# A steady state with a ring of three PSUM banks and GpSimd in VectorE's place, in a fused attention and linear layer

## The chip, the core and the metric

The kernel runs on one core of a Trainium2 chip. The metric is the device time of one execution in microseconds (us), the median of three runs. The engines are TensorE (PE, matrix products from SBUF into PSUM), VectorE (DVE), ScalarE (ACT), GpSimd (POOL) and SyncE (SP, which here issues every DMA). Each engine takes its instructions in the order in which they were written; semaphores tie the engines together. PSUM has eight banks of 128 partitions x 512 f32.

## What is computed

The input is x of shape (8, 1024, 256). It is normalised over the last axis; an attention layer and a quantised linear layer both read the result and are added to x:

```python
xn = _layernorm(x, axis=-1)
x = x + attn(xn, Wq, Wk, Wv, Wo, bo) + ffn(xn, weight_q, weight_scale, bias)

# attn: 16 heads of 16, 8 KV heads, so a group is 2 heads
energy = einsum('nqhd,nkhd->nhqk', q, k) + alibi_bias   # -|i-j| * 2**-(h+1)
p = softmax(energy / sqrt(16)); out = einsum('nhqk,nkhd->nqhd', p, v) @ Wo.T + bo
# ffn: int8 quantisation of xn per token, product with int8 weights, scales, bias
x_scale = max(amax(|x|), 1e-6) / 127; x_q = clip(round(x / x_scale), -128, 127)
out = (x_q @ weight_q.T) * x_scale * weight_scale + bias
```

## The kernel before, in words

The 8192 tokens are 64 tiles of 128 (index t). The attention is 64 units (index u): one batch element and one KV head, so two query heads e = 0, 1 over 1024 x 1024 scores. A unit has 8 key blocks c of 128 keys and, with e, 16 slots s = 2c + e. While unit u runs, one tile is prepared (t = u + PREP_AHEAD, 11 ahead) and one finished (u - OUT_BEHIND, 9 behind), so that the steady state does four things together.

**Column blocks** (`col_block`, L919): scores transposed, 128 keys x 512 queries a half h, a half to one PSUM bank. There are two banks, `ps_col[h]`. q and k are split into bf16 parts, so that one bf16 product of 122 rows gives nearly f32 scores; the bias and minus the row maximum are among these rows. The product is issued in four strips of 32 weights (`in_strips`, L880). ACT takes the exp of each half into `probs` (L797), which frees the bank (`exp_done`). POOL multiplies the block on the diagonal by a factor (`weigh_near`, L516).

**pv blocks** (`pv_block`, L936): four f32 products a block c, with the column of sums included, accumulated into `ps_pv`. After block 7, DVE transposes `ps_pv` in 32 x 32 blocks (`turn_pv`, L655, semaphore `pv_read`), and later divides and transposes again (`norm`, L662, semaphore `att_unit_ready`). The next unit's pv block 0 waits for `pv_read`.

**Row blocks** (`row_block`, L887): the scores of later heads (numbers 2u+3 and 2u+4, 8 blocks each, so 16 per unit) with the queries on partitions, 128 x 1024, into `ps_row[qb % 2]`, only for the row maxima. DVE reduces each (`reduce_block`, L631, L635), and a row block waits until the reduce two blocks before is done (`row_max_found`). `split_max` (L638) writes the negated maxima as two bf16 numbers, PE turns them (`turn_max`, L897), ACT keeps them (`keep_max_t`, L774) and SP writes them into rows of q_col (`place_max`, L336).

**Preparation and finishing**: statistics, `normalise`, `find_scale`, `quantise` (DVE, L546 to L585), products in f32 with all 128 weights for q, k, v (`make_qkv`, L829), bf16 for the linear part (`make_lin`, L847), splitting of q and k into three parts (ACT `keep_qkv`, `find_middle`, DVE `find_rest`, POOL `find_low`), and for the finished tile the projection (`project`, L948) and `finish` (DVE, L683). All of them share one bank, `ps_work`, one after the other.

SP's queue for unit u (L407) is, in this order: the next tile of x, att_t of the tile to be finished, the column set of unit u+1 (10 DMAs; it waits until PE has ended the unit before), `place_max` of head 0, `store_out`, `place_max` of head 1, the row set of unit u+3 (10 DMAs, after the scores that used its buffer), `store_parts`, `store_att(u-1)`. PE's first column block of a unit waits for the column set of 14 DMAs, the four of `place_max` among them (L965).

The order of PE's and DVE's work in a unit is written by slots (L961, L692). PE issues the row blocks in pairs after even slots, pv block c-1 or so in odd ones, the projection at s = 6, turning xn at 8, qkv at 10 between the two row blocks, turning xq at 12, the linear product at 14. DVE does two reduces at each even slot, and turn_pv at s = 1, statistics 5, split_max 6, finish, normalise and find_scale 7, quantise 9, find_rest and norm 11, split_max 14, scale_lin 15.

Of the kernel before, what the change touches and what calls it, by code (L numbers as in the profile page):

```python
# [62 lines left out]
PREP_AHEAD = 11  # L63
OUT_BEHIND = 9
RING = 32
# [4 lines left out]
SLOTS = 2 * BLOCKS  # L70

# [22 lines left out]
def build(nc, x, wqk_t, wv_t, wo_t, w8_t, w_scale, bias_attn, bias_lin, q_alibi, k_alibi, diag,  # L94
          eye, parts_dram, att_dram, out):
    ctx = ExitStack()
    with ctx:
# [33 lines left out]
        parts = sb("parts", [P, 2, PARTS, QK_CHUNKS * P], BF16)  # L131
        lin = sb("lin", [P, 2, EMBED])
        v_all = sb("v_all", [P, RING, P])

# [21 lines left out]
        ps_col = [ctx.enter_context(nc.psum_tensor(f"ps_col{i}", [P, HALF], F32)) for i in range(2)]  # L156
        ps_pv = ctx.enter_context(nc.psum_tensor("ps_pv", [P, HALF], F32))
        ps_work = ctx.enter_context(nc.psum_tensor("ps_work", [P, HALF], F32))

        early = [(ps_row[i][:, 0:HALF], ps_row[i][:, HALF:SEQ]) for i in range(2)]  # L160
        work = (ps_work[:, :], ps_work[:, :])

        def last_bank(t):


            banks = [ps_row[i][:, h * HALF:(h + 1) * HALF] for i in range(2) for h in range(2)]
            banks += [ps_col[0], ps_col[1], ps_pv, ps_work]
            return banks[t % BLOCKS][:, 0:EMBED]
# [38 lines left out]
        col_scores = sem("col_scores")  # L207
        exp_done = sem("exp_done")
# [10 lines left out]
        att_last_loaded = [sem(f"att_last_loaded{i}") for i in range(EC)]  # L219
        projected = sem("projected")  # L220
        out_ready = sem("out_ready")
        out_stored = [sem(f"out_stored{i}") for i in range(2)]
# [10 lines left out]
        def wait_apart(eng, s, value):  # L233
# [9 lines left out]
        SEGMENTS = [  # L243
            (0, 1, True, False, False, 2, True),
            (1, OUT_BEHIND, True, True, False, 2, True),
            (OUT_BEHIND, UNITS - PREP_AHEAD, True, True, True, 2, True),
            (UNITS - PREP_AHEAD, UNITS - 3, False, True, True, 2, True),
            (UNITS - 3, UNITS - 2, False, True, True, 2, False),
            (UNITS - 2, UNITS - 1, False, True, True, 1, False),
            (UNITS - 1, UNITS, False, True, True, 0, False),  # L250
        ]
        def run_units(eng, unit):


            for first, end, prep, prev, proj, row_heads, row_set in SEGMENTS:
                flags = dict(prep=prep, prev=prev, proj=proj, row_heads=row_heads, row_set=row_set)
# [18 lines left out]

        def row_banks_spare(f, s):

            return f["row_heads"] == 0 or (f["row_heads"] == 1 and s >= BLOCKS)

        def col_bank(f, s, h):  # L280

            if row_banks_spare(f, s) and s % 2:
                return ps_row[0][:, h * HALF:(h + 1) * HALF]
            return ps_col[h][:, :]
# [5 lines left out]
        def _(sp):  # L290
# [45 lines left out]
            def place_max(u, par, e):  # L336

                wait_apart(sp, max_t_ready, GROUP * u + e + 1)
# [16 lines left out]
            def load_att_t(t, par):  # L355

                wait_apart(sp, att_stored, 16 * GROUP * (t + BLOCKS))
                wait_apart(sp, projected, t)
                sp.dma_start(att_t[:, par, :, :], att_dram[:, bass.ds(t * P, P)].rearrange(
                    "(c p) n -> p c n", p=P)).then_inc(att_t_loaded, 16)  # L360
# [7 lines left out]
            sp.dma_start(base[:, 1:PREP_AHEAD, :],  # L368
                         x[P:PREP_AHEAD * P, :].rearrange("(t p) d -> p t d", p=P)).then_inc(
# [14 lines left out]
            def next_x(t):  # L384

                wait_apart(sp, x_loaded, 16 * (t - PREP_AHEAD))
# [20 lines left out]
            def unit(u, par, f):  # L407
                if f["prep"]:
                    if f["proj"]:

                        wait_apart(sp, out_ready, u - OUT_BEHIND)
                    next_x(u + PREP_AHEAD)
                if f["proj"]:
                    load_att_t(u - OUT_BEHIND, (par + OUT_BEHIND) % 2)
                not_last = not (isinstance(u, int) and u == UNITS - 1)
                if not_last:

                    wait_apart(sp, col_scores, 2 * SLOTS * u)
                    load_col_set(u + 1, 1 - par)
                    place_max(u + 1, 1 - par, 0)  # L420
                if f["proj"]:
                    store_out(u - OUT_BEHIND, (par + OUT_BEHIND) % 2)
                if not_last:
                    place_max(u + 1, 1 - par, 1)
                if f["row_set"]:

                    wait_apart(sp, row_scores, BLOCKS * GROUP * (u + 2))
                    if f["prep"]:
                        wait_parts(u + PREP_AHEAD, (par + PREP_AHEAD) % 2)
                    else:  # L430
                        wait_parts(TILES, 0)
                    load_row_set(u + 3, 1 - par)
                if f["prep"]:
# [10 lines left out]
            load_att_t(TILES - OUT_BEHIND, (TILES - OUT_BEHIND) % 2)  # L444

# [7 lines left out]
            for t in range(TILES - OUT_BEHIND, TILES):  # L453
                sp.wait_ge(out_ready, t + 1)
# [7 lines left out]
        def _(pool):  # L462
# [53 lines left out]
            def weigh_near(u, c):  # L516

                wait_apart(pool, exp_done, 2 * SLOTS * u + 2 * GROUP * (c + 1))
# [3 lines left out]

            def unit(u, par, f):
                t, tpar = u + PREP_AHEAD, (par + PREP_AHEAD) % 2
                for c in range(BLOCKS):
                    weigh_near(u, c)
                    if c == 1 and not (isinstance(u, int) and u == UNITS - 1):
# [3 lines left out]
                    if c == 2 and f["prep"]:  # L531
                        find_rstd(t, tpar)
                    if c == 6 and f["prep"]:
                        find_low(t, tpar)
                if f["prep"]:
                    add_linear(t, tpar)

            run_units(pool, unit)


# [520 lines left out]
```

## Time and profile before

| | |
|---|---|
| median of 3 runs | 1769.76 us (1768.62 to 1770.13) |
| profiled execution | 1769.02 us |
| its span in the trace | 1767.2 us |
| instructions | 68604 |
| mean granted TensorE clock | 0.988 |
| HBM read, written | 101.06 MB, 35.65 MB |

The span is what the trace covers; the profiled execution is 1.8 us longer. A page of the profile gives the busy time of each engine; the chain of waits follows back from the last instruction to what released it; the timeline lists instructions in order of time, merged where they follow each other ("x8" is eight instructions, the second column their common duration). Starts are us from the span's start. Matmul durations include the drain of the array and overlap, so the cost of a matmul on PE is read from the distance of starts or from the chain, not from its duration.

### The profile page before, as it was taken

To read this page: it belongs to the slowest core of one execution; us is meant where nothing else is said; L and a number is where in the kernel's file an instruction comes from. 1 tells how busy PE (TensorE), PEld (TensorE's weight loads), DVE (VectorE), ACT (ScalarE), POOL (GpSimd) and SP (SyncE) were. 2 spreads that over 40 slices of the span, in tenths; PEclk is the share of its full clock that TensorE was granted. 3 is DMA by queue.
4 is the path that set the end of the run, shared out by engine and by line. 5 is a ranking of instruction groups with operands and counts; after the bars stand their busy time and mean duration, and the time that the engine had idled before them with its cause. 6 is when DMAs were issued, how large, how long until landed. Compare 5 with 4: busy or idle time off the path is not lost.

```text
span 1767.2 us, 68604 instructions
## 1 busy us (share of the span) xinstructions
PE 1707.5 (97%) x22272; PEld 719.4 (41%) x22272; DVE 1594.3 (90%) x2306; ACT 1243.0 (70%) x2498; POOL 591.9 (33%) x904
## 2 busy tenths in 40 slices
PE   6799999999999999999999999999999999999997
PEld 4234443443443443443443443443444444333333
DVE  6899999999999999999999999999999999999991
ACT  3267777777777777777777777777777777777775
POOL 4323333333333333333333333333333333222221
PEclk9799999999999999999999999999999999999999
DMA  4322223223223223223223223223233222222222
GB/s 117 86 71 76 65 70 80 71 79 86 75 78 85 76 78 85 75 79 85 75 79 84 74 81 84 74 81 83 75 81 84 74 81 80 71 72 68 72 63 70
DMA packets 184331, 137.99 MB, mean 78 GB/s; under 512 B 102649, under 2 KB 143865, under 8 KB 184281
## 3 DMA queue, kind: packets, MB, share of 16 engines
q1 hardware_dynamic: 184280, 137.34, 28.8%
q8 instruction: 29, 0.48, 0.1%
q14 instruction: 22, 0.17, 0.0%
HBM read 101.06 MB, written 35.65 MB: 77 GB/s over the span
## 4 chain that ended last, share of the span: by engine, by line
PE 69%; DVE 19%; issue 7%; DMA 1%; DVEq 1%; ACT 1%; SPq 1%; POOL 0%; POOLq 0%; ACTq 0%
PE ps_row L884 20%; PE ps_col L884 19%; PE ps_pv L943 18%; DVE row_max L635 13%; PE ps_work L833 5%; PE ps_work L950 3%; DVE att_normed L674 2%; DVE rest L591 2%; PE ps_work L836 1%; PE ps_work L825 1%; PE ps_work L850 1%; ACT probs L797 1%; DVE rsum L667 1%; DMA bias<-bias_lin 0%; DVEq L231 0%
## 5 line engine op out<-in xcount | busy, mean ns | idle before, releaser
L797 ACT ACTIVATE probs<-ps_col 128x512 f32<-128x512 f32 x2024 | 1098.4, 595 | 293.4 <-PE ps_col L884 293.0
L635 DVE TENSOR_REDUCE row_max<-ps_row 128x1 f32<-128x1024 f32 x1024 | 1201.2, 1213 | 64.4 <-PE ps_row L884 62.8
L520 POOL TENSOR_TENSOR probs<-probs,near 128x256 f32<-128x256 f32 x512 | 376.8, 736 | 1074.0 <-ACT probs L797 1074.0
L884 PE MATMUL ps_col<-q_col,k_col 122*32 122x512 bf16 x8096 | 657.0, 383 | 0.5 <-ACT probs L797 0.4
L884 PE MATMUL ps_row<-k_row,q_row 120*32 120x512 bf16 x8192 | 579.0, 386 | 23.2 <-DVE row_max L635 18.2
L943 PE MATMUL ps_pv<-probs,v_unit 128*32 128x512 f32 x4096 | 530.9, 594 | 3.1 <-POOL probs L520 2.9
L884 PEld LDWEIGHTS ps_col<-q_col,k_col 122*32 122x32 bf16 x8096 | 202.7, 94 | 548.3 <-ACT probs L797 428.6
L884 PEld LDWEIGHTS ps_row<-k_row,q_row 120*32 120x32 bf16 x8192 | 193.5, 95 | 212.7 <-DVE row_max L635 139.6
L943 PEld LDWEIGHTS ps_pv<-probs,v_unit 128*32 128x32 f32 x4096 | 119.6, 110 | 82.4 <-issue 11.9
L833 PE MATMUL ps_work<-xn_t,wqk 128*128 128x128 f32 x636 | 85.1, 284 | 0.0
L833 PEld LDWEIGHTS ps_work<-xn_t,wqk 128*128 128x128 f32 x636 | 75.0, 191 | 22.5 <-issue 22.5
L744 ACT ACTIVATE v_all<-ps_work 128x128 f32 (+1 forms) x53 | 14.7, 277 | 89.8 <-PE ps_work L836 89.8
L660 DVE STREAM_TRANSPOSE pv_turned<-ps_pv 128x512 f32<-128x512 f32 x64 | 45.2, 706 | 20.4 <-PE ps_pv L943 20.4
L950 PE MATMUL ps_work<-wo,att_t 128*128 128x256 f32 x224 | 63.3, 405 | 0.0
L781 ACT ACTIVATE neg_max_t<-ps_work 16x128 bf16<-16x128 bf16 x128 | 34.0, 266 | 37.4 <-PE ps_work L899 34.3
L481 POOL TENSOR_TENSOR parts<-rest,parts 128x384 bf16<-128x384 f32 x64 | 59.1, 923 | 0.9 <-ACT parts L753 0.7
L490 POOL TENSOR_TENSOR base<-base,lin 128x256 f32 (+1 forms) x64 | 46.8, 731 | 11.6 <-POOL base L488 11.2
L488 POOL TENSOR_TENSOR base<-base,bias 128x256 f32 (+1 forms) x64 | 47.1, 736 | 9.7 <-DVE lin L598 8.0
L950 PEld LDWEIGHTS ps_work<-wo,att_t 128*128 128x128 f32 x224 | 37.9, 189 | 27.1 <-issue 24.2
L689 DVE TENSOR_TENSOR out_tile<-ps_work,base 128x256 f32<-128x256 f32 x55 | 23.4, 425 | 20.9 <-issue 15.9
L739 ACT ACTIVATE xn_t<-ps_work 128x256 f32<-128x256 f32 x53 | 20.3, 383 | 29.8 <-PE ps_work L825 29.8
L475 POOL TENSOR_TENSOR rstd<-rstd,half_pow 128x1 f32<-128x1 f32 x64 | 35.8, 559 | 11.9 <-POOL rstd L472 11.0
(74 smaller groups left out, 807.4 us busy)
## 6 DMA issues: line engine op xcount, KB each, us to landing
parts_dram<-parts SPq DMA_DIRECT2D x64, 288.0 KB, 3.2
q_row<-parts_dram SPq DMA_DIRECT2D x128, 96.0 KB
q_col<-parts_dram SPq DMA_DIRECT2D x128, 96.0 KB
q_row<-parts_dram SPq DMA_DIRECT2D x128, 64.0 KB
q_col<-parts_dram SPq DMA_DIRECT2D x128, 64.0 KB
att_dram<-att_unit SPq DMA_DIRECT2D x128, 64.0 KB
att_t<-att_dram SPq DMA_DIRECT2D x56, 128.0 KB, 2.2
out<-out_tile SPq DMA_DIRECT2D x55, 128.0 KB, 1.8
```

The costliest lines, as they stand in the source:

```text
L475: pool.tensor_tensor(rstd[:, par, 1:2], rstd[:, par, 0:1], half_pow[:, :], ALU.pow).then_inc(rstd_ready, 1)
L481: pool.tensor_tensor(parts[:, par, 2, :], rest[:, par, :], parts[:, par, 1, :], ALU.subtract).then_inc(low_ready, 1)
L488: pool.tensor_tensor(here, here, bias[:, :], ALU.add).then_inc(base_ready, 1)
L490: pool.tensor_tensor(here, here, lin[:, par, :], ALU.add).then_inc(base_ready, 1)
L520: pool.tensor_tensor(here, here, near[:, bass.ds(u % KV_HEADS, 1), :].rearrange("p a (e n) -> p (a e) n", e=GROUP), ALU.mult).then_inc(wei ...
L635: dve.tensor_reduce(row_max[:, e, qb:qb + 1], ps_row[qb % 2][:, :], AX_X, ALU.max).then_inc(row_max_found, 1)
L660: dve.transpose(pv_turned[:, :], ps_pv[:, :]).then_inc(pv_read, 1)
L797: act.activation(probs[:, c % PBUFS, e, h * HALF:(h + 1) * HALF], col_bank(f, s, h), ACT.Exp, scale=SCALE).then_inc(exp_done, 1)
L833: pe.matmul(bank[:, m * P:(m + 1) * P], wqk[:, c, m * P:(m + 1) * P], xn_t[:, c, :], start=(c == 0), stop=(c == EC - 1))
L884: mm = pe.matmul(to[at, :], weights[:, at], moving, start=start, stop=stop)
L943: mm = pe.matmul(ps_pv[32 * j:32 * j + 32, :], v_unit[:, par, c, :], probs[:, c % PBUFS, j // 2, (j % 2) * HALF:(j % 2 + 1) * HALF], start ...
L950: mm = pe.matmul(bank, att_of_tile[:, c, :], wo[:, c, :], start=(c == 0), stop=(c == EC - 1))
```

## The change

**Ring.** The three banks of ps_col and ps_work become three of one kind, `ps_ring`, and every product of the steady state that isn't a row block or a pv block takes the next of them in a fixed order: 32 column halves and four further items, "early_max" after c = 2, "turns" after 5, "qkv" after 6, "outputs" after 7. An item waits until the item three before it is freed by ACT (`ring_freed`). Turns holds xn, xq and the maxima of head 1; outputs holds the linear product and the projection. ACT copies what it holds to SBUF (`keep_turns`, `keep_qkv_whole`, `keep_outputs`; three, two and two copies) in the order of the ring. Items that have nothing to do in the first or last units are filled and freed by small instructions. The products of the preparation keep their 128 weights; they aren't cut into strips.

**PE's order** in block c: half (e 0, h 0), half (0, 1), row block 2c, half (1, 0), pv block c-2 (for c = 0, 1 blocks 6, 7 of the unit before), half (1, 1), row block 2c+1, and then the further item.

**DVE** keeps two reduces per c (now negated by the reduce itself), and behind them: statistics at c = 0, turn_pv at c = 1, normalise and find_scale at c = 2, norm at c = 3. **POOL** gets split_max, quantise, the split of q and k (`split_qk`, one unit later than before), the weighting of the linear product, and finish. ACT scales the linear product by the token's scale.

**SP's order**: next x (one tile further ahead), att_t, column set, store_parts of the tile before, place_max of head 0, store_att(u-1), row set, store_out of the tile before, place_max of head 1.

```diff
+    others = {2: "early_max", 5: "turns", 6: "qkv", 7: "outputs"}
+    for c in range(BLOCKS):
+        items += [(c, e, h) for e in range(GROUP) for h in range(2)]
+        if c in others:
+            items.append(others[c])
```

In SP's `unit(u, par, f)`:

```diff
+                if not f["last"]:
+
+                    wait_apart(sp, ring_filled, ITEMS * u)
                     load_col_set(u + 1, 1 - par)
+                if f["lag"]:
+                    store_parts(u + PREP_AHEAD - 1, (par + PREP_AHEAD - 1) % 2)
+                if not f["last"]:
                     place_max(u + 1, 1 - par, 0)
-                if f["proj"]:
-                    store_out(u - OUT_BEHIND, (par + OUT_BEHIND) % 2)
-                if not_last:
-                    place_max(u + 1, 1 - par, 1)
+                if f["prev"]:
+                    store_att(u - 1)
                 if f["row_set"]:
                     wait_apart(sp, row_scores, BLOCKS * GROUP * (u + 2))
...
                     load_row_set(u + 3, 1 - par)
-                if f["prep"]:
-                    store_parts(u + PREP_AHEAD, (par + PREP_AHEAD) % 2)
-                if f["prev"]:
-                    store_att(u - 1)
+                if f["out"]:
+                    store_out(u - OUT_BEHIND - 1, (par + OUT_BEHIND + 1) % 2)
+                if not f["last"]:
+                    place_max(u + 1, 1 - par, 1)
```

In POOL's:

```diff
+                if f["prev"] and not f["last"]:
+                    split_max(GROUP * u + 2, 0)
+                if f["lag"]:
+                    split_qk(t - 1, 1 - tpar)
                 for c in range(BLOCKS):
                     weigh_near(u, c)
+                    if c == 0 and f["prep"]:
+                        find_rstd(t, tpar)
+                    if c == 1 and f["lag"]:
+                        weigh_linear(t - 1, 1 - tpar)
+                        add_linear(t - 1, 1 - tpar)
...
                     if c == 2 and f["prep"]:
+                        quantise(t, tpar)
+                    if c == 3 and f["row_heads"] >= 1:
+                        split_max(GROUP * u + 3, 1)
+                    if c == 3 and f["out"]:
+                        finish(u - OUT_BEHIND - 1, (par + OUT_BEHIND + 1) % 2)
```

In DVE's:

```diff
+                for c in range(BLOCKS):
+                    for i in (2 * c, 2 * c + 1):
+                        if i < BLOCKS and f["row_heads"] >= 1:
+                            reduce_block(GROUP * u + 3, 1, i)
+                        if i >= BLOCKS and f["row_heads"] >= 2:
+                            reduce_block(GROUP * u + 4, 0, i - BLOCKS)
+                    if c == 0 and f["prep"]:
+                        wait(dve, x_loaded, 16 * (t - X_AHEAD + 1))
+                        find_stats(t, tpar)
+                    if c == 1 and f["prev"]:
                         turn_pv(u - 1)
+                    if c == 2 and f["prep"]:
                         normalise(t, tpar)
                         find_scale(t, tpar)
+                    if c == 3 and f["prev"]:
                         norm(u - 1)
```

In PE's program:

```diff
+            def take_bank(u, item):
+                if not (isinstance(u, int) and ITEMS * u + PLACE[item] < BANKS):
+                    pe.wait_ge(ring_freed, ITEMS * u + PLACE[item] - BANKS + 1)
+                return ring_bank(item)
+            def unit(u, par, f):
+                for c in range(BLOCKS):
+                    if c == 0:
+                        pe.wait_ge(col_set_loaded[par], 16 * COL_SET * ((u - par) // 2 + 1))
+                    col_half(u, par, c, 0, 0)
+                    col_half(u, par, c, 0, 1)
+                    ahead_row_block(u, par, f, 2 * c)
+                    col_half(u, par, c, 1, 0)
+                    if c >= 2:
+                        pv_block(u, par, c - 2)
+                    elif f["prev"]:
+                        pv_block(u - 1, 1 - par, BLOCKS - 2 + c)
+                    col_half(u, par, c, 1, 1)
+                    ahead_row_block(u, par, f, 2 * c + 1)
```

## Rows read from the trace of the kernel before

**Rows 1.** The page: busy us (share of the span) x instructions, by engine.
```profile
PE 1707.5 (97%) x22272; PEld 719.4 (41%) x22272; DVE 1594.3 (90%) x2306; ACT 1243.0 (70%) x2498; POOL 591.9 (33%) x904
```

**Rows 2.** Chain of waits, 903 to 930 us: start, length, what.
```profile
905.05 2.33 DVE row_max L635 x2
...
907.42 0.61 PE ps_row L884 x8
908.04 0.33 PE ps_work L850 x2
...
908.91 0.86 PE ps_pv L943 x8
...
910.28 0.86 PE ps_row L884 x16
...
919.43 1.06 PE ps_work L950 x4
...
923.28 0.37 PE ps_work L825 x2
```

**Rows 3.** Timeline of DVE in the same unit: start, length, line, operation.
```profile
903.66 0.24 DVE L667 RECIPROCAL rsum<-pv_turned 128x16 f32<-128x16 f32 x1
...
913.14 0.70 DVE L660 STREAM_TRANSPOSE pv_turned<-ps_pv 128x512 f32<-128x512 f32 x1
913.77 2.31 DVE L635 TENSOR_REDUCE row_max<-ps_row 128x1 f32<-128x1024 f32 x2
...
918.55 0.42 DVE L548 BATCH_NORM_STATS2 stats<-base 128x6 f32 x1
...
919.23 2.35 DVE L635 TENSOR_REDUCE row_max<-ps_row 128x1 f32<-128x1024 f32 x2
...
922.72 0.41 DVE L558 TENSOR_SCALAR xn<-base,mean_var,rstd 128x256 f32 x1
...
923.97 2.36 DVE L635 TENSOR_REDUCE row_max<-ps_row 128x1 f32<-128x1024 f32 x2
926.25 0.34 DVE L577 TENSOR_SCALAR xclip<-xn,xinv 128x256 f32<-128x256 f32 x1
...
928.59 1.22 DVE L635 TENSOR_REDUCE row_max<-ps_row 128x1 f32<-128x1024 f32 x1 [0.21 <-PE ps_row L884]
```

**Rows 4.** Timeline of PE, the row blocks on both sides of qkv.
```profile
925.41 0.61 PE L884 MATMUL ps_row<-k_row,q_row 120*32 120x512 bf16 x8
...
927.92 0.62 PE L884 MATMUL ps_row<-k_row,q_row 120*32 120x512 bf16 x8
```

**Rows 5.** DVE's transposes of ps_pv: all, and two of the drain.
```profile
L660 DVE STREAM_TRANSPOSE pv_turned<-ps_pv x64: 703/706/717, 122.0 to 1749.4; 128x512 f32<-128x512 f32 x64
...
1496.87 0.71 DVE L660 STREAM_TRANSPOSE pv_turned<-ps_pv 128x512 f32<-128x512 f32 x1
...
1520.62 0.71 DVE L660 STREAM_TRANSPOSE pv_turned<-ps_pv 128x512 f32<-128x512 f32 x1
```

**Rows 6.** Groups by line: two-input operations of POOL, busy us, mean ns.
```profile
L481 POOL TENSOR_TENSOR parts<-rest,parts 128x384 bf16<-128x384 f32 x64 | 59.1, 923 | 0.9 <-ACT parts L753 0.7
...
L488 POOL TENSOR_TENSOR base<-base,bias 128x256 f32 x60 | 44.1, 735 | 6.8 <-DVE lin L598 5.1
```

**Rows 7.** Timeline of SP's queue, 923 to 938 us.
```profile
923.93 0.40 SPq L440 DMA_DIRECT2D out<-out_tile  x1
925.53 1.35 SPq L340 DMA_DIRECT2D q_col<-neg_max_t  x2
927.77 1.74 SPq L319 DMA_DIRECT2D k_row<-parts_dram  x3
...
934.33 0.31 SPq L326 DMA_DIRECT2D k_row<-k_alibi  x1
...
936.13 1.58 SPq L351 DMA_DIRECT2D att_dram<-att_unit  x2
```

**Rows 8.** The page's DMA issues: KB each, us from issue to landing.
```profile
out<-out_tile SPq DMA_DIRECT2D x55, 128.0 KB, 1.8
```

More of the change, by code:

```diff
@@ L239, in wait_apart, with flags_of @@
                 eng.sem_inc(waited, 1)
[L243 to L251, printed above, removed]
+        SEGMENTS = [(0, 1), (1, OUT_BEHIND), (OUT_BEHIND, OUT_BEHIND + 1), (OUT_BEHIND + 1, 52),
+                    (52, 53), (53, 54), (54, 60), (60, 61), (61, 62), (62, 63), (63, 64)]
+        def flags_of(u):
+            return dict(
+                prep=u + PREP_AHEAD < TILES,
+                lag=0 < u and u - 1 + PREP_AHEAD < TILES,
+                prev=u > 0,
+                proj=u >= OUT_BEHIND,
+                out=u > OUT_BEHIND,
+                next_x=u + X_AHEAD < TILES,
+                row_heads=max(0, min(GROUP, UNITS - 1 - u)),
+                row_set=u + 3 < UNITS,
+                last=u == UNITS - 1,
+            )
         def run_units(eng, unit):
-            for first, end, prep, prev, proj, row_heads, row_set in SEGMENTS:
-                flags = dict(prep=prep, prev=prev, proj=proj, row_heads=row_heads, row_set=row_set)
+            for first, end in SEGMENTS:
+                flags = flags_of(first)
+                assert all(flags_of(u) == flags for u in range(first, end))
                 if end - first == 1:
@@ L800, in unit @@
[L800 to L815 removed]
+                keep_first_max(e)
@@ new lines, in qkv_whole @@
+            def qkv_whole(u, par):
+                t, bank = u + PREP_AHEAD, take_bank(u, "qkv")
+                pe.wait_ge(xn_t_ready, t + 1)
+                for m in range(QK_CHUNKS):
+                    for c in range(EC):
+                        pe.matmul(bank[:, m * P:(m + 1) * P], wqk[:, c, m * P:(m + 1) * P],
+                                  xn_t[:, c, :], start=(c == 0), stop=(c == EC - 1))
+                for c in range(EC):
+                    mm = pe.matmul(bank[:, QK_CHUNKS * P:], xn_t[:, c, :], wv[:, c, :],
+                                   start=(c == 0), stop=(c == EC - 1))
+                mm.then_inc(ring_filled, 1)
@@ new lines, in outputs @@
+            def outputs(u, par, f):
+                t, bank = u + PREP_AHEAD, take_bank(u, "outputs")
+                if f["prep"]:
+                    pe.wait_ge(xq_t_ready, t + 1)
+                    for c in range(EC):
+                        mm = pe.matmul(bank[:, 0:EMBED], xq_t[:, c, :], w8[:, c, :],
+                                       start=(c == 0), stop=(c == EC - 1))
+                if f["proj"]:
+                    pe.wait_ge(att_t_loaded, 16 * (u - OUT_BEHIND + 1))
+                    opar = (par + OUT_BEHIND) % 2
+                    for c in range(EC):
+                        mm = pe.matmul(bank[:, EMBED:2 * EMBED], att_t[:, opar, c, :], wo[:, c, :],
+                                       start=(c == 0), stop=(c == EC - 1))
+                else:
+                    mm = pe.transpose(max_turn(bank), eye_b[:, 0:MAX_ROWS * BLOCKS], eye_b[:, :])
+                mm.then_inc(ring_filled, 1)
@@ L948, in project @@
+            run_units(pe, unit)
+            for c in (BLOCKS - 2, BLOCKS - 1):
+                pv_block(UNITS - 1, (UNITS - 1) % 2, c)
             def project(att_of_tile, bank):
```

401 lines of the change are left out of this document (222 added, 179 removed).

## Prediction

> **What bounds the kernel now.** I read the page's busy line first [rows 1]. TensorE (PE) is busy 97% of the span, VectorE (DVE) 90%, ScalarE (ACT) 70%, GpSimd (POOL) 33%. That says PE and DVE are both near the limit, but not which wait matters, so next I read the chain of waits over one unit of the steady state [rows 2] and DVE's timeline of the same unit [rows 3]. The reader is to see a loop through two engines. A row block (two 512-wide score products in four strips, 0.86/2 = 0.43 us) fills one of two ps_row banks, DVE reduces it, and only then may PE fill that bank again. Three constants of this loop follow. From PE's start of a row block to DVE's start on it: 928.59 - 927.92 = 0.67 us [rows 3, 4]. From one reduce to the next: (926.25 - 923.97)/2 = 1.14 us [rows 3]. From the start of a reduce to the next use of its bank: two reduces started at 905.05, the second ended 2.33 later and PE went on at 907.42, so 2.37 - 1.14 = 1.23, and with the 0.03 that waits add elsewhere I use 1.26 us [rows 2].
>
> The unit's length comes from DVE's transposes of ps_pv, one per unit [rows 3, 5], the first at 122.0: 1496.87 - 913.14 = 583.7 us for 22 units, 26.53 us each. The first 30 take 791.1 us; with 22 of 26.53 the 8 units without projection take 25.9 each. Without preparation a unit takes 1520.62 - 1496.87 = 23.75 us.
>
> PE's own work in a full unit: eight column blocks c, each of four column halves (0.85), two row blocks (0.86) and one pv block (0.86): 2.56 us, so 20.5. Beside them projection 1.06, the linear product 0.33, turning xn 0.37 [rows 2], qkv 927.92 - 925.41 - 0.43 = 2.08 [rows 4], small turns 0.2. Sum 24.5 us; 2 us of the 26.53 are waits.
>
> **The change, DVE and PE.** DVE loses quantise, the splits of the maxima, rest, the scaling of the linear product and finish. What it keeps beside 16 reduces (18.2 us) has four terms [rows 3]: statistics 919.23 - 918.55 = 0.68; the transpose of ps_pv 913.77 - 913.14 = 0.63; normalise and scale 923.97 - 922.72 = 1.25; norm 905.05 - 903.66 = 1.39 [rows 2, 3]. Sum 22.2 us, below PE's 24.5. On the sum alone both engines have room. But the change also moves the terms: all four now stand behind the reduces of c = 0, 1, 2 and 3, while all of PE's extras stand at the ends of c = 5 (turns), 6 (qkv) and 7 (outputs). In c = 0 to 3 DVE has 8 x 1.14 + 3.95 = 13.1 us of work against PE's 10.3, and two banks let DVE lag by one block only. In c = 5 to 7 DVE starves. So I worked the loop through. R is PE's start of a row block, D the start of its reduce, us from the unit's first matmul. Between R of an even and of the next odd block PE does 1.71 us, between odd and even 0.85.
>
> R0 0.43, D0 1.10. R1 2.14, D1 2.81. Statistics push D2 to 4.63; D3 5.77. The transpose runs 6.91 to 7.61. Here a new wait bites: pv block 0 now stands in c = 2 and needs that transpose (pv_read). PE comes to it at 6.53 and is held to 7.66, with row block 5 queued behind it. R5 8.73, D4 7.54, D5 9.40. Normalise and scale to 11.79, D6 11.79, D7 12.93. R8 is wanted at 12.19 and must wait for D6 + 1.26 = 13.05. Norm runs 14.07 to 15.5. D8 15.46, so R10, wanted at 15.61, waits until 16.72. From there PE works alone: R11 18.43, turns 0.52, R12 19.80, R13 21.9, qkv, R14 24.7, R15 26.5, outputs to 28.25. In this stretch 0.5 us is the ring: turns, qkv and outputs occupy ring banks for three, two and two ACT copies at some 0.50 each (1243.0 us over 2498 instructions, [rows 1]), and the third column half behind them needs the bank. So 28.25 us by PE and DVE, where it was 26.53.
>
> What the ring gives: a part of the 2 us of waits is column halves that wait for the exp of their bank; with three banks a half needs the exp of three items back, which at 0.50 each is done. In c = 0 to 3 that gain lies under DVE's loop and vanishes there.
>
> **The change, GpSimd.** POOL takes over quantise (3 operations), the splits (4 short), high, rest and middle of qk (3 of 384 columns), the weighting of the linear product and finish. No row shows one-input operations of these sizes on POOL; from above they are bounded by its two-input ones, 0.73 for 256 columns and 0.92 for 384 [rows 6], from below by half that. With 8 weighings of 0.73, low, add_linear and the rest POOL has between 14 and 20 us per unit; I take 17.5. It fits into 28. What is queued: split_max and split_qk stand in front of weigh_near of c = 0, about 5 us from the unit's start, with weigh_near done near 5.8. Its product pv 0 is due at 6.5 and held to 7.66 anyway. Covered, by 1.9 us. The rows show POOL at 0.73 us for 256 columns of two inputs [rows 6] and DVE at 0.34 for the clip of as many with one, at 926.25 [rows 3]. The Trainium skill, GPSIMD Engine Reference (its introduction and "Elementwise — side-by-side cycle accounting"), calls GpSimd the wrong choice for ordinary elementwise arithmetic, about two times slower than VectorE. DVE gives up about 2.7 us a unit (1594.3/64 = 24.9 [rows 1], less the 22.2 it keeps). By that rule they become an estimated 5.4 on POOL, inside the 14 to 20 that the rows give; the sum is the same by both unless POOL comes late, which is a part of rival B.
>
> ACT loses middle (0.5) and gains two copies of 256 columns (0.8): no bound.
>
> **The change, SP's queue.** This is the step on which the size depends. The first product of a unit waits for its whole column set, of which the last transfers are the maxima of head 1 (place_max(u+1, 1)). Before, these were issued ahead of the row set. Now SP goes: column set, store_parts, place_max 0, store_att(u-1), row set, store_out, place_max 1. store_att waits for norm, and norm stands in c = 3, ready at 15.5 plus 0.1 for waking PE from a DMA: 15.6. Everything queued behind it waits too. Prices [rows 7]: store_att 1.58; the gap of waits in front of the row set 927.77 - (925.53 + 1.35) = 0.89; row set (934.33 + 0.31) - 927.77 = 6.87; store_out 0.40; the first of the two place_max transfers 1.35/2 = 0.67; the second lands about 1.9 after its issue (a transfer to the output 1.8 [rows 8]; none of 2 KB has a row, bounds 1.0 and 3.0); three short gaps of 0.4 (estimate, bounds 0.1 and the 0.89 just named). Sum 13.5 us. Unit: 15.6 + 13.5 = 29.1 us. That is later than PE's own 28.25, so this chain sets the end and PE idles 0.8 us at the head of a unit. The gap fits the other moves: store_parts comes one unit later, and the wait for stored parts ends before 15.6.
>
> **Sum**, against the profiled execution's 1769.0 us (span 1767.2 and 1.8 around it; the median of the runs is 1769.8). Units 9 to 52: 44 x (29.1 - 26.53) = +113. Units 1 to 8, no store_out in the chain: 28.3 against 25.9, 8 x 2.4 = +19. Units 53 to 60, no statistics and no normalise, so norm ends at 14.2, but the row set is still issued: 27.7 against 23.75, 8 x 3.95 = +32. Unit 0 has neither transpose nor norm, -2.5. The last three have no row set, -1. Together +160: 1930 us.
>
> **Rivals.**
> (A) SP's chain is shorter than I price it (landing at 1.0, gaps at 0.1) and PE with DVE sets the unit: 28.25 for units 9 to 52 (+76), 27.2 for 1 to 8 (+10), 23.6 in the drain (-1), -3.5 at the ends. 1851 us. For it: 0.8 us of difference hangs on one landing I can't see. Against: each listed transfer has a measured price.
> (B) A landing of 3 us behind the row set's packets, or POOL late, delaying weigh_near and pv in c = 0 to 3: another 1.0 us for 60 units, 1990 us.
> (C) The other side, faster. Mechanism: DVE's lag is absorbed and PE's work decides, at 24.5 us. It decides only if DVE's c = 0 to 3 fitted beside PE's, and the shortest loop I can write says no: D0 to D8 13.1, to the reuse of the bank 1.26, PE from R10 to the next R0 11.4, and 0.67: 26.4 us, even with no pv_read wait, no idle of DVE between D0 and D1 and no ring wait. So faster asks that a constant of mine is over by 10%. If it did decide: 1769 - 2.0 x 60 = 1650 us.
> (D) The loop at its floor, 26.4, SP hidden: 1765 us, no change.
>
> **How the numbers follow.** Forecast (SP chain) 0.50; A 0.25; B 0.15; C 0.05; D 0.05. The forecast's own range is 1890 to 1965 (landing and gaps at their ends, 0.7 us for 60 units). To leave out 2 in 10 the range goes from 1845, just under A, to 1990, at B. A measurement of this kernel can tell about 0.2% (3.5 us) from no change. Faster: C and a part of D, 0.06. Same 0.03. Slower 0.91.
>
> **What would show it.** In the profile after: PE at the first column half of a unit idle about 1 us, released by the q_col<-neg_max_t transfer; SP waiting about 4 us ahead of store_att in each unit; PE's pv at c = 2 held by pv_turned for about 1 us; row blocks 8 and 10 waiting about 1 us for row_max, none waiting in c = 5 to 7; DVE's busy share near 77%, PE's 84%. If DVE's idle is spread evenly over the unit, or the units without preparation stay at 23.7 us, the argument on SP is wrong. If a full unit is under 26.4 us, the loop is wrong.

## The result

| | before | after |
|---|---|---|
| median | 1769.76 us | 1920.53 us (1918.37 to 1927.12, 4 runs) |
| ratio | | 1.086, 95% interval 1.083 to 1.089 |
| span of the profiled execution | 1767.2 us | 1916.2 us (execution 1918.37) |

The change makes the kernel 8.6% slower. The page after answers to [rows 1]: busy us, share and instructions by engine, and the shares of the chain that ended last.

```profile
PE 1699.2 (89%) x22294; PEld 782.0 (41%) x22294; DVE 1444.1 (75%) x1736; ACT 1273.7 (66%) x2575; POOL 973.6 (51%) x1580
...
PE 27%; SPq 26%; issue 20%; DVE 18%; DMA 6%; DVEq 1%; ACT 1%; POOL 0%; POOLq 0%; ACTq 0%
```

VectorE is relieved as meant, by 150 us of busy time, and yet no engine is busier than PE at 89%. SP's queue, which only issues DMAs, has 26% of the chain. The transposes of ps_pv give the length of the units, as [rows 5] did. Timeline of DVE: units 1, 9, 53 and 61.

```profile
125.57 0.71 DVE L753 STREAM_TRANSPOSE pv_turned<-ps_pv 128x512 f32<-128x512 f32 x1
...
349.94 0.71 DVE L753 STREAM_TRANSPOSE pv_turned<-ps_pv 128x512 f32<-128x512 f32 x1
...
1618.98 0.70 DVE L753 STREAM_TRANSPOSE pv_turned<-ps_pv 128x512 f32<-128x512 f32 x1
...
1839.63 0.71 DVE L753 STREAM_TRANSPOSE pv_turned<-ps_pv 128x512 f32<-128x512 f32 x1
```

Units 1 to 8 take 28.05 us on average (25.9 before), units 9 to 52 28.84 (26.53), units 53 to 60 27.58 (23.88). That is 17 + 102 + 30 = 149 us, as much as the difference of the spans; what comes before the first transpose (3.6 us more) and behind the last (less) nearly cancels.

Timeline of SP in one unit, to be laid beside [rows 7]:

```profile
1015.75 0.32 SPq L358 DMA_DIRECT2D k_col<-k_alibi  x1
1016.43 0.66 SPq L329 DMA_DIRECT2D parts_dram<-parts  x1
1017.73 1.47 SPq L376 DMA_DIRECT2D q_col<-neg_max_t  x2
1023.52 1.55 SPq L387 DMA_DIRECT2D att_dram<-att_unit  x2
1026.05 1.75 SPq L351 DMA_DIRECT2D k_row<-parts_dram  x3
1028.19 4.25 SPq L351 DMA_DIRECT2D q_row<-parts_dram  x6
1032.61 0.31 SPq L358 DMA_DIRECT2D k_row<-k_alibi  x1
1033.22 0.40 SPq L474 DMA_DIRECT2D out<-out_tile  x1
1033.81 1.52 SPq L376 DMA_DIRECT2D q_col<-neg_max_t  x2
```

SP stands idle from 1019.2 to 1023.5 and then issues to 1035.3, with one gap of 1.0 us, in front of the row set, and shorter ones. Timelines of DVE and PE around it, with the idle time in brackets:

```profile
1022.62 0.45 DVE L774 STREAM_TRANSPOSE att_unit<-att_normed 128x256 f32<-128x256 f32 x1
```

```profile
1007.47 0.72 PE L1003 MATMUL ps_ring<-q_col,k_col 122*32 122x512 bf16 x8 [0.32 <-DMA q_col<-neg_max_t]
...
1010.52 0.70 PE L1003 MATMUL ps_row<-k_row,q_row 120*32 120x512 bf16 x8
...
1015.44 1.06 PE L1056 MATMUL ps_pv<-probs,v_unit 128*32 128x512 f32 x8 [1.10 <-DVE pv_turned L753]
...
1020.80 0.61 PE L1003 MATMUL ps_row<-k_row,q_row 120*32 120x512 bf16 x8 [0.39 <-DVE row_max L730]
...
1024.23 0.62 PE L1003 MATMUL ps_row<-k_row,q_row 120*32 120x512 bf16 x8 [0.66 <-DVE row_max L730]
...
1036.50 0.62 PE L1003 MATMUL ps_ring<-q_col,k_col 122*32 122x512 bf16 x8 [0.52 <-DMA q_col<-neg_max_t]
```

The unit starts at 1007.47; norm ends at 1023.07, 15.60 us later; SP's chain ends with PE's start at 1036.50, 13.43 us after that. Inside, PE waits for the transpose at pv block 0 and for reduces at row blocks 8 and 10, as the hand schedule has it.

### The profile page after: what moved, and what is told of

Read it like the earlier page. It is cut to its first block, busy times and chain, and to the rows that moved or that the text cites. A ratio compares the mean times of both kernels' runs of the same rounds, so it can differ in the third digit from the quotient of the medians.

```text
span 1916.2 us, 68781 instructions
## 1 busy us (share of the span) xinstructions
PE 1699.2 (89%) x22294; PEld 782.0 (41%) x22294; DVE 1444.1 (75%) x1736; ACT 1273.7 (66%) x2575; POOL 973.6 (51%) x1580
## 4 chain that ended last, share of the span: by engine, by line
PE 27%; SPq 26%; issue 20%; DVE 18%; DMA 6%; DVEq 1%; ACT 1%; POOL 0%; POOLq 0%; ACTq 0%
SPq L351 16%; PE ps_pv L1056 9%; DVE row_max L730 9%; PE ps_row L1003 8%; PE ps_ring L1003 8%; DMA q_col<-neg_max_t 5%; SPq L387 4%; SPq L376 2%; DVE att_normed L767 1%; DVE amax L660 1%; DVE xn L653 1%; DVE att_unit L774 1%; DVE stats L643 1%; SPq L474 1%; DVE pv_turned L753 1%
## 5 line engine op out<-in xcount | busy, mean ns | idle before, releaser
L865 ACT ACTIVATE probs<-ps_ring 128x512 f32<-128x512 f32 x2048 | 1130.3, 596 | 375.7 <-PE ps_ring L1003 345.2
L1003 PE MATMUL ps_ring<-q_col,k_col 122*32 122x512 bf16 x8192 | 749.2, 382 | 47.6 <-DMA q_col<-neg_max_t 42.1
L1003 PE MATMUL ps_row<-k_row,q_row 120*32 120x512 bf16 x8192 | 645.6, 386 | 73.5 <-DVE row_max L730 63.3
L1056 PE MATMUL ps_pv<-probs,v_unit 128*32 128x512 f32 x4096 | 535.8, 594 | 64.0 <-DVE pv_turned L753 34.2
L1003 PEld LDWEIGHTS ps_ring<-q_col,k_col 122*32 122x32 bf16 x8192 | 234.1, 95 | 413.4 <-ACT probs L865 126.8
L570 POOL TENSOR_SCALAR xclip<-xn,xinv 128x256 f32<-128x256 f32 x53 | 60.9, 1149 | 74.0 <-DVE xinv L666 74.0
L1096 PE MATMUL ps_ring<-xn_t,wqk 128*128 128x128 f32 x636 | 85.1, 284 | 0.0
L1096 PEld LDWEIGHTS ps_ring<-xn_t,wqk 128*128 128x128 f32 x636 | 75.0, 191 | 22.5 <-ACT probs L865 22.5
L753 DVE STREAM_TRANSPOSE pv_turned<-ps_pv 128x512 f32<-128x512 f32 x64 | 45.2, 706 | 25.9 <-PE ps_pv L1056 25.9
L573 POOL TENSOR_SCALAR xround<-xclip 128x256 f32<-128x256 f32 x53 | 57.2, 1079 | 9.8 <-POOL xclip L570 9.5
L1114 PE MATMUL ps_ring<-wo,att_t 128*128 128x256 f32 x220 | 57.7, 385 | 0.0
L586 POOL TENSOR_TENSOR rest<-qk,parts 128x384 f32<-128x384 f32 x53 | 48.8, 921 | 9.5 <-POOL parts L584 9.3
L577 POOL TENSOR_SCALAR xq<-xround 128x256 bf16<-128x256 f32 x53 | 46.1, 870 | 14.5 <-POOL xround L573 14.3
L525 POOL TENSOR_TENSOR base<-base,lin 128x256 f32 (+1 forms) x64 | 46.7, 729 | 13.4 <-POOL base L523 12.9
```

The costliest lines, as they stand in the source:

```text
L570: pool.tensor_scalar(xclip[:, :], xn[:, par, :], xinv[:, par, :], Q_MAX, ALU.mult, ALU.min).then_inc(xq_ready, 1)
L753: dve.transpose(pv_turned[:, :], ps_pv[:, :]).then_inc(pv_read, 1)
L865: act.activation(probs[:, c % PBUFS, e, h * HALF:(h + 1) * HALF], ring_bank((c, e, h)), ACT.Exp, scale=SCALE).then_inc(ring_freed, 1)
L1003: mm = pe.matmul(to[at, :], weights[:, at], moving, start=start, stop=stop)
L1056: mm = pe.matmul(ps_pv[32 * j:32 * j + 32, :], v_unit[:, par, c, :], probs[:, c % PBUFS, j // 2, (j % 2) * HALF:(j % 2 + 1) * HALF], start ...
L1096: pe.matmul(bank[:, m * P:(m + 1) * P], wqk[:, c, m * P:(m + 1) * P], xn_t[:, c, :], start=(c == 0), stop=(c == EC - 1))
```

## Experiments

Theory S says that SP's chain from norm to place_max sets the unit; theory D says that the bunching of DVE's work against PE's extras does. The first three runs bear on the two, one edit each; the fourth prices the third bank.

**e1: store_att behind place_max.**

```diff
-                if f["prev"]:
-                    store_att(u - 1)
                 if f["row_set"]:
...
                     place_max(u + 1, 1 - par, 1)
+                if f["prev"]:
+                    store_att(u - 1)
```

> The changed kernel with one edit: in SP's queue store_att(u-1) moves from ahead of the row set to behind place_max of head 1, so nothing of the next unit's column set waits for norm. Theory S (SP's chain norm, store_att, row set, store_out, place_max sets the unit at 28.84 us, PE and DVE follow at about 28.4): PE no longer waits for q_col<-neg_max_t; full units go to about 28.4, units without projection to 27.3, drain units from 27.6 to about 23.7; total 1863 us. Theory D (the bunched DVE work alone sets the unit, SP's wait is a by-product): full units unchanged at 28.8, total above 1900.

Measured 1869.6 us, 1.056 (1.054 to 1.058) of before. So 51 of the 151 us go when SP no longer waits for norm ahead of the next unit's set. The row for PE's wait on q_col<-neg_max_t, 42.1 us over 57 times after, is gone from the list of waits. Units 9 to 52 take 28.38 us on average (28.34 from the transpose at 1027.60 to the one at 1055.94). So S sets the end, and D stands 0.5 us behind it, which is why the unit gained only so little and the drain, where D gives 24.6 us, gained most: 24 us over 8 units, against 20 over the 44 full ones.

**e2: norm one block later, SP's queue as changed.**

```diff
-                    if c == 3 and f["prev"]:
+                    if c == 4 and f["prev"]:
                         norm(u - 1)
```

> The changed kernel with one edit: DVE's norm(u-1) moves from behind the reduces of c = 3 to behind those of c = 4; SP's queue stays. Theory S: norm ends 2.4 us later, and everything behind store_att with it: about 31.2 us a unit, total near 2065. Theory D: DVE's work of c = 0 to 3 shrinks by 1.39 us, so row block 10 waits no longer and the unit falls to about 27.6, total near 1860. The two have opposite signs against 1920.

Measured 2184.2 us, 1.235 (1.232 to 1.237). The sign is S's and the size nearly twice the forecast, 264 us instead of 145. Timeline of PE, two starts of a unit, then the stretches around the second: us, busy of PE, PEld, DVE, ACT, POOL, granted clock, DMA share, GB/s.

```profile
1004.43 1.15 PE L1003 MATMUL ps_ring<-q_col,k_col 122*32 122x512 bf16 x8 [3.51 <-DMA q_col<-neg_max_t]
...
1010.04 0.66 PE L1003 MATMUL ps_row<-k_row,q_row 120*32 120x512 bf16 x8
...
1038.54 1.04 PE L1003 MATMUL ps_ring<-q_col,k_col 122*32 122x512 bf16 x8 [3.66 <-DMA q_col<-neg_max_t]
```

```profile
1005.00:1010.00 5.00, 5.00 (x48) 2.73 (x42) 1.35 (x2) 2.28 (x4) 0.38 (x2) 0.53 0.36 105
1010.00:1015.00 5.00, 3.78 (x62) 1.79 (x56) 4.84 (x7) 3.85 (x7) 3.02 (x6) 1.00 0.32 89
1015.00:1020.00 5.00, 4.88 (x69) 1.84 (x69) 4.01 (x7) 3.22 (x7) 2.81 (x5) 1.00 0.21 47
...
1035.00:1040.00 5.00, 1.46 (x16) 0.72 (x20) 0.00 (x0) 1.54 (x4) 3.22 (x6) 0.70 0.24 75
1040.00:1045.00 5.00, 5.00 (x54) 1.75 (x48) 2.33 (x2) 2.31 (x5) 0.74 (x1) 0.62 0.38 101
```

The end of norm in between, from DVE's timeline:

```profile
1024.64 0.45 DVE L774 STREAM_TRANSPOSE att_unit<-att_normed 128x256 f32<-128x256 f32 x1
```

This unit is 34.1 us; units 9 to 52 average 33.3. Norm ends at 1025.09, 20.66 after the start instead of the 18.0 expected, and 13.45 later PE starts: SP's chain is as long as in the changed kernel. Of the missing 2.7 us nearly all is the clock: after 3.5 us without work PE runs at a granted 0.53, close to the lower of its two levels (1.2 of 2.4 GHz). From the first column half to row block 2 it takes 1010.04 - 1004.43 = 5.6 us; the changed kernel took 1010.52 - 1007.47 = 3.05, at a granted 1.00. That makes 2.6 us. The wait lengthens the path that leads to the wait.

**e3: transpose of ps_pv between the reduces of c = 1.**

```diff
                             reduce_block(GROUP * u + 4, 0, i - BLOCKS)
+                        if i == 2 and f["prev"]:
+                            turn_pv(u - 1)
...
-                    if c == 1 and f["prev"]:
-                        turn_pv(u - 1)
```

> The changed kernel with one edit: DVE's transpose of ps_pv moves between the two reduces of c = 1, so that it ends before PE comes to pv block 0. Theory S and theory D both lose the wait of pv block 0 (1.1 us): norm ends 0.7 us earlier after the unit's start, 0.7 us a unit, total near 1878. Rival W (the pv_read wait is covered by DVE's backlog, since row blocks wait for reduces anyway): under 0.2 us a unit, total above 1908.

Measured 1870.0 us, 1.056 (1.054 to 1.058). Units 9 to 52 take 28.06 us, 0.78 less. In the changed kernel PE stood idle for 64.0 us in all in front of pv blocks, of which the profile puts 34.2 down to pv_turned; here it is 0.0. So this wait cost some 50 us; W falls.

**e4: two banks.** `BANKS = 2`, three banks allocated.

> The changed kernel with a ring of two banks in place of three, all else as it is. What the third bank is worth here. Theory S: in c = 0 to 3 the added waits lie under DVE's loop; in c = 5 to 7 a column half waits for turns, qkv and outputs, PE's own unit grows from 28.4 by about 2 us and passes SP's chain: 30 to 30.5 us a unit, total near 2010. Rival H (the waits are hidden below SP's chain): within 5 us of 1920.

Measured 2015.3 us, 1.138 (1.136 to 1.140): a unit of 30.3 us. PE's timeline shows where: the half behind turns, qkv and outputs.

```profile
1014.14 0.40 PE L1003 MATMUL ps_ring<-q_col,k_col 122*32 122x512 bf16 x4 [0.66 <-ACT neg_max_t L871]
...
1019.58 0.40 PE L1003 MATMUL ps_ring<-q_col,k_col 122*32 122x512 bf16 x4 [0.57 <-ACT qk L894]
...
1024.25 0.40 PE L1003 MATMUL ps_ring<-q_col,k_col 122*32 122x512 bf16 x4 [0.59 <-ACT proj L909]
```

The third bank is no by-product: in this order of work it is worth 95 us. This prices a bank in the ring, not the ring against the layout of before, which had three banks too, one of them set aside for the further items; no run compares those.

**e5 to e7: both chains loosened.** In e5, store_att last as above, and norm at c = 6:

```diff
-                    if c == 3 and f["prev"]:
+                    if c == 6 and f["prev"]:
                         norm(u - 1)
```

> The changed kernel with store_att last in SP's queue and, beside it, norm behind the reduces of c = 6, where PE makes qkv. By the loop of row blocks and reduces (theory S + D): the waits of row blocks 10 go, a full unit takes 27.1 us, total near 1796. If DVE's bunching were not the second limit, it would stay at the value of e1_store_att_last, 1863 or so.

Measured 1831.4 us, 1.035 (1.033 to 1.037). Norm's place costs 38 us once SP doesn't wait for it; with SP waiting, moving it by one block cost 264. With the transpose moved as well (e6):

> As e5_store_last_norm_c6, and the transpose of ps_pv between the two reduces of c = 1. Expected: the wait of pv block 0 goes, row block 8 still waits 1.0 us for DVE; a full unit takes 26.4 us, total near 1757, about 0.7% below the kernel before. If the transpose were covered, no change from e5.

Measured 1789.4 us, 1.012 (1.010 to 1.013). Both effects came with their signs; both totals are 32 to 35 us over the forecast, and e6, forecast 0.7% faster than the kernel before, is 1.2% slower. In e6 normalise takes 0.66 us beside POOL instead of 0.41, row block 8 waits 0.8, and weight loads of pv blocks wait 26.3 us in 52 waits for weigh_near, which stands behind quantise on POOL. Waits of e6 (total, times, longest), and its timelines of DVE and POOL:

```profile
PEld ps_pv L1056 <- POOL probs L555: 26.3, 52, 0.6
```

```profile
1014.78 0.66 DVE L653 TENSOR_SCALAR xn<-base,mean_var,rstd 128x256 f32 x1
```

```profile
1014.56 0.73 POOL L555 TENSOR_TENSOR probs<-probs,near 128x256 f32<-128x256 f32 x1
```

And with two banks again (e7):

> As e6_and_turn_early with a ring of two banks. With the two chains above gone, this prices the third bank where PE sets the unit: expected about 2 us a unit, total near 1865. If the third bank gave nothing, it would stay at e6's value.

Measured 1923.7 us, 1.088 (1.086 to 1.089): the third bank is worth 134 us here, 2.0 us a unit (29.03 against 27.02).

**e8: DVE's steps spread.** On top of e6: each of DVE's steps where PE has its extras, and on POOL (not shown) find_rstd and the linear steps at c = 5 and quantise in three pieces at c = 0, 1, 2.

```diff
-                    if c == 0 and f["prep"]:
-                        wait(dve, x_loaded, 16 * (t - X_AHEAD + 1))
-                        find_stats(t, tpar)
+                    if c == 4 and f["next_x"]:
+                        wait(dve, x_loaded, 16 * (t + 1 - X_AHEAD + 1))
+                        find_stats(t + 1, 1 - tpar)
...
-                    if c == 2 and f["prep"]:
-                        normalise(t, tpar)
-                        find_scale(t, tpar)
+                    if c == 7 and f["next_x"]:
+                        normalise(t + 1, 1 - tpar)
+                        find_scale(t + 1, 1 - tpar)
```

> As e6_and_turn_early, and DVE's preparation steps moved to where PE has its extras: statistics of the next tile at c = 4, norm at c = 6, normalise and find_scale of the next tile at c = 7; on POOL find_rstd of the next tile at c = 5, the three steps of quantise one each at c = 0, 1, 2, and the linear steps at c = 5. If bunching on DVE is what holds a unit of e6 at 27.1 us, no row block waits for a reduce for long and PE's own work of 24.5 plus about 0.7 of ring waits sets the unit: 25.3 us, total near 1695, 4% below the kernel before. If something else holds it (POOL's total, ring), it stays above 26.5 us a unit, total above 1755.

Measured 1725.4 us, 0.975 (0.974 to 0.977): faster than before. A unit is 25.7 us, 0.4 over the forecast. Two limits of e6 went together: PE's waits for row_max fell from 45.6 to 7.7 us, and those of the pv blocks' weight loads for weigh_near from 26.3 to 0.4. The run doesn't say how the 64 us divide between DVE's steps and POOL's. PE still waits 15.8 us in all for q_col<-neg_max_t. SP's issues fill 19.1 us of a unit; between them it waits for no engine, only for two transfers of its own (waits of SP's queue, 800 to 1100 us: total, times, longest):

```profile
SPq L274 <- DMA att_dram<-att_unit: 12.2, 12, 1.3
SPq L274 <- DMA parts_dram<-parts: 5.4, 11, 0.5
```

**e11: the load of att_t behind the column set.** On top of e8:

```diff
-                if f["proj"]:
-                    load_att_t(u - OUT_BEHIND, (par + OUT_BEHIND) % 2)
                 if not f["last"]:
                     wait_apart(sp, ring_filled, ITEMS * u)
                     load_col_set(u + 1, 1 - par)
+                if f["proj"]:
+                    load_att_t(u - OUT_BEHIND, (par + OUT_BEHIND) % 2)
```

> As e8_dve_spread, and in SP's queue the load of att_t moves from ahead of the column set to behind it. In e8 SP waits 1.0 us a unit for att_dram<-att_unit to land, which it had issued just before, and place_max of head 1 lands as PE comes to the next unit (issued 1013.3, PE starts at 1015.2 where it could at 1014.9). If SP's queue is what e8's units of 25.6 us follow, the wait goes and a unit falls to about 25.1: total near 1700. If PE's own waits for the ring set it, no change: 1725.

Measured 1706.3 us, 0.9645 (0.963 to 0.966) of before, the fastest of all. PE's wait on q_col is gone; a unit is 25.48 us, from transpose to transpose:

```profile
1013.61 0.70 DVE L768 STREAM_TRANSPOSE pv_turned<-ps_pv 128x512 f32<-128x512 f32 x1
1039.09 0.70 DVE L768 STREAM_TRANSPOSE pv_turned<-ps_pv 128x512 f32<-128x512 f32 x1
```

```profile
900.00:1100.00 200.00, 199.84 (x2739) 92.29 (x2735) 177.21 (x204) 152.23 (x314) 128.83 (x205) 1.00 0.31 83
```

PE is busy 199.84 of 200 us here, against 182.43 in the changed kernel in the same stretch (a busy PE includes the drains of its matmuls).

**e12: what the relief is worth.** In the version of e11 quantise goes back to DVE, behind the reduces of c = 3:

> As e11_att_load_later, with one part of VectorE's relief undone: the three steps of quantise go back from POOL to DVE, together behind the reduces of c = 3, 0.91 us of DVE time by the rows of before. What this part of the relief is worth once the order is right. If DVE's lag of one block absorbs it (0.7 us of slack), PE's own work still sets the unit: 25.5 us, within 8 us of e11's 1706. If the relief is what lets PE run, a unit grows by 0.5 us or more: above 1730.

Measured 1738.5 us, 0.9825 (0.981 to 0.984): 32 us slower than e11. A unit takes 26.07 us instead of 25.47. The second case of the expectation came: this part of the relief is worth something in the order of e11. What it is worth in the order of the changed kernel, no run shows.

**e9: POOL's load, in the changed kernel.** The three steps of quantise with `[:, 0:16]` in place of whole rows, so most of the quantised input isn't computed.

> The changed kernel with the three steps of quantise on POOL cut to 16 of 256 columns, so most of the quantised input of the steady state isn't computed: 2.6 us of POOL time less per unit, nothing else changed. Theory S: POOL is covered, within 4 us of 1920. Rival P (POOL's slow elementwise work delays weigh_near and finish, and with them the unit): at least 0.4 us a unit, below 1897.

Measured 1924.5 us (1918.9 to 1925.5), 1.087 (1.085 to 1.088), the changed kernel's time. POOL is busy for 2.1 us less in a unit (the expectation said 2.6) without any gain, so quantise is covered there and P falls. Its other new work, ahead of the weighing of block 0, is covered too by the trace of the changed kernel: that weighing ends at 1012.27, and PE comes to pv block 0 at 1014.17 only, where it then waits for the transpose.

**e10: SP's order alone, in the kernel before.**

```diff
-                if f["proj"]:
-                    store_out(u - OUT_BEHIND, (par + OUT_BEHIND) % 2)
-                if not_last:
-                    place_max(u + 1, 1 - par, 1)
+                if f["prev"]:
+                    store_att(u - 1)
                 if f["row_set"]:
...
-                if f["prev"]:
-                    store_att(u - 1)
+                if f["proj"]:
+                    store_out(u - OUT_BEHIND, (par + OUT_BEHIND) % 2)
+                if not_last:
+                    place_max(u + 1, 1 - par, 1)
```

> The kernel before with one edit: SP's queue of a unit gets the order of the changed kernel, place_max of head 0, store_att(u-1), row set, store_parts, store_out, place_max of head 1. Nothing else of the change is in. There norm ends 22.1 us after a unit's start (before: 905.1 against 883.1). Theory S: 22.1 + 13.4 + 0.9 for store_parts = 36.4 us a unit, and about 2.8 more since PE, idle for over 3 us at the head of a unit, ran the next 5 us at a granted clock of 0.5 to 0.6 in e2_norm_c4: 36 to 39 us, total between 2350 and 2550. Theory D (SP's order costs nothing by itself): 1770.

Measured 2470.9 us, 1.396 (1.394 to 1.399). Timelines of PE, DVE and SP:

```profile
994.23 1.04 PE L884 MATMUL ps_col<-q_col,k_col 122*32 122x512 bf16 x8 [9.71 <-DMA q_col<-neg_max_t]
...
1033.44 1.05 PE L884 MATMUL ps_col<-q_col,k_col 122*32 122x512 bf16 x8 [9.88 <-DMA q_col<-neg_max_t]
```

```profile
1018.47 0.45 DVE L681 STREAM_TRANSPOSE att_unit<-att_normed 128x256 f32<-128x256 f32 x1
```

```profile
1019.35 1.54 SPq L351 DMA_DIRECT2D att_dram<-att_unit  x2
...
1030.72 1.54 SPq L340 DMA_DIRECT2D q_col<-neg_max_t  x2
```

From the end of norm, 1018.92, to PE's start 14.5 us; this order of SP alone costs 40%. The chain is that of the changed kernel (13.4) with store_parts in it; what differs is when norm ends in the unit, 24.7 us after its start here and 15.6 there. The unit starts at a granted clock of 0.50 (994 to 999 us), after 9.7 us of idle time.

## Why the prediction was right

The forecast was 1930 us, the measured time is 1920.5, and the case is the one named likeliest, SP's chain.

- **Units.** 29.1, 28.3 and 27.7 us were forecast for units 9 to 52, 1 to 8 and 53 to 60; 28.84, 28.05 and 27.58 came. The units bring 16 us less than forecast, and the two ends of the run 4 us more (+1 where -3.5 was forecast).
- **Units 53 to 60** came out right in the mean partly by luck. I had them alike, norm's end 14.2 and SP's chain 13.5. From transpose to transpose they take 25.5 to 29.7 us. In those that start at 1725 to 1807 norm ends some 14.4 us after the start and the chain takes 13.0, 27.4 together. In those that start at 1666.63 and 1696.02, after 3.5 and 3.3 us of idle time, the first 5 us run at a granted clock of 0.66, and norm ends 15.8 and 16.2 us after the start. My sum has no term for the clock; a shorter chain and, in two units, a slower start made up for each other. I also took 23.75 us from one unit of the drain before; eight of them average 23.88. Timeline of PE in the changed kernel, two starts of units in the drain, and the stretches behind them:

```profile
1666.63 1.05 PE L1003 MATMUL ps_ring<-q_col,k_col 122*32 122x512 bf16 x8 [3.54 <-DMA q_col<-neg_max_t]
...
1725.29 0.62 PE L1003 MATMUL ps_ring<-q_col,k_col 122*32 122x512 bf16 x8 [2.82 <-DMA q_col<-neg_max_t]
```

```profile
1666.00:1671.00 5.00, 4.37 (x48) 1.75 (x52) 1.35 (x2) 2.25 (x4) 0.00 (x0) 0.66 0.30 82
...
1725.00:1730.00 5.00, 4.71 (x72) 2.14 (x76) 3.10 (x3) 3.75 (x7) 0.74 (x1) 1.00 0.34 94
```

- **SP's chain** was worked out at 13.5 us from the end of norm and is 13.43. Of its two terms without a row of their own, the landing of 2 KB, put at 1.9, is 1.74 in the chain of waits, and 1.91 from its issue to PE's start; the three short gaps, put at 1.2, are 0.94.
- **Norm's end** was put at 15.5, 15.6 with 0.1 for PE's waking, and is 15.60. The exact match is luck, two errors that cancel: the unit's first reduces start 0.2 us later, and norm takes 1022.99 - 1021.79 = 1.20 instead of 1.39, since att_normed takes 0.43, where in the unit of [rows 3] it took 0.62 beside a POOL operation.
- **PE and DVE by themselves** were put at 28.25; e1 gives 28.38. The terms, with what the changed kernel shows: the wait of pv block 0 1.13 (wanted at 1014.17, started at 1015.44: 1.27); row block 8 0.86 (wanted at 1020.23, started at 1020.80: 0.57), row block 10 1.11 (0.83). The two row waits were over-sized by 0.3 each, so some 0.5 us that the hand schedule doesn't have lie elsewhere. A part may be the ring, which no run isolates: I priced a copy at 0.50, the mean of all of ACT's instructions, and the exp of a half takes 0.60 in both kernels. PE's idle time at the head, 0.8 forecast, is 0.3 to 0.5.
- **GpSimd** was the step with a wrong premise. I bounded its one-input operations from above by its two-input ones, 0.73 us. They take 1.15, 1.08 and 0.86 by the profile, whose spans on POOL are rough; the casts of 384 columns only 0.50. That the sum came out near all the same (112.03/200 x 28.84 = 16.2 us a unit against 17.5) is luck. The cover held, as e9 shows for quantise. In e6 it no longer did.

```profile
1019.96 1.15 POOL L570 TENSOR_SCALAR xclip<-xn,xinv 128x256 f32<-128x256 f32 x1 [1.44 <-DVE xinv L666]
1021.30 1.08 POOL L573 TENSOR_SCALAR xround<-xclip 128x256 f32<-128x256 f32 x1 [0.19 <-POOL xclip L570]
1022.66 0.86 POOL L577 TENSOR_SCALAR xq<-xround 128x256 bf16<-128x256 f32 x1 [0.29 <-POOL xround L573]
```

- **The Trainium skill's rule** for elementwise arithmetic (GPSIMD Engine Reference, introduction: VectorE is roughly two times faster) is too mild for these three: DVE took 0.34 for the clip [rows 3], POOL 1.15, 3.4 times as long. It changes nothing in the sum here, since that time is spare.
- **Busy shares**: DVE 75% (77 forecast), PE 89% (84 forecast; a busy PE includes the drains of its matmuls, so idle time of under 1 us is partly hidden in it).
- **The ring** was said to gain nothing in c = 0 to 3. That nearly holds: with two banks (e4) norm ends 16.3 us after the start, 0.7 later, and 0.6 of it is the wait of the unit's second half for proj, the last row shown there. But I didn't weigh what two banks would cost with the further items in the same ring: 95 us.

So the mechanism was right, and it is the likeliest case of the forecast that came; taken away, it gives back only a third of the loss, since the loop of PE and DVE lies 0.5 us behind it. The other mechanisms stand behind the first in a row, each step a run: SP's order (51 us), then norm and the transpose (38 and 42 us, e5 and e6), which together undo 131 of the 151 us; then the rest of DVE's bunching together with POOL's (64 us, one run, not divided), and SP's wait for its own store (19 us).

What stays open: how e11's remaining 1.0 us a unit over PE's own 24.5 divides between ring waits and the small ones. No run takes the ring waits away alone, and none moves DVE's steps of e8 without POOL's.

## What to carry to other kernels

Sums per engine said that this change had room everywhere; it lost 8.6% because moved work was put where its neighbour was already the limit, and because one DMA queue had a late wait ahead of transfers that the next unit needs. When steps are moved, write the schedule of one period out with two engines side by side, and for each in-order DMA queue ask what is behind every wait and when that is needed. The same work in the best order tried is 3.5% faster than the kernel before. There the relief pays (32 us for quantise), and the third bank of the ring is worth more (134 us in e6's order, 95 in the changed kernel's).

## What the runs showed of the hardware

- PE idle for 3.5 us at the start of a unit ran the next 5 us at a granted clock of 0.53 (e2), and for 9.7 us at 0.50 (e10). In the drain of the changed kernel 3.5 and 3.3 us of idle time gave 0.66, and four starts after 2.7 to 2.8 us stayed at 1.00, as did those after 0.3 to 0.5 us in its full units. A wait at the head of a period can thus cost more than its length: in e2 2.6 us on top of 3.5.
- DVE's att_normed, with two inputs in SBUF, takes 0.42 us alone. Where it runs into a two-input operation on POOL it ends 0.3 us after that one: in the unit of [rows 3] at 904.56 (POOL's at 904.26), so it took 0.62; in e12 at 1001.68 (POOL's at 1001.40), so it took 0.97. POOL's operation takes its 0.73 either way. Beside the one-input rounding on POOL, in the changed kernel at 1022.07, att_normed took 0.43. The Trainium skill, GPSIMD Engine Reference, "Specifications", names this contention for DVE instructions with two SBUF inputs or in a 2-port perf mode; for the two inputs the traces agree. Normalise has one input in SBUF beside its values per row, and in e6 it ended at 1015.44, behind POOL's 1015.29; in which mode it ran, no trace shows. Timelines of DVE and POOL, before and e12:

```profile
903.94 0.62 DVE L674 TENSOR_TENSOR att_normed<-pv_turned,rsum 128x256 f32<-128x256 f32 x1
```

```profile
903.53 0.73 POOL L520 TENSOR_TENSOR probs<-probs,near 128x256 f32<-128x256 f32 x1 [4.03 <-ACT probs L797]
```

```profile
1000.71 0.97 DVE L776 TENSOR_TENSOR att_normed<-pv_turned,rsum 128x256 f32<-128x256 f32 x1
```

```profile
1000.67 0.73 POOL L556 TENSOR_TENSOR probs<-probs,near 128x256 f32<-128x256 f32 x1
```
